# Phase 0 of a two-FFN transformer layer: block 1's mixing ahead of block 2's statistics, the first merged matrices among the r matmuls of the last block

## The reference

```python
x = x + 0.5 * ffn(layernorm(x))          # phases 0 and 3: the same W_r, W_k, W_v, mu_r, mu_k
x = x + attn_layer(layernorm(x))         # phases 1 and 2
x = x + 0.5 * ffn(layernorm(x))

def ffn(z):                              # z_prev: z shifted by one token
    xr = mu_r * z + (1 - mu_r) * z_prev
    xk = mu_k * z + (1 - mu_k) * z_prev
    r = sigmoid(xr @ W_r.T)
    return r * (square(relu(xk @ W_k.T)) @ W_v.T)

def attn_layer(h):                       # 16 heads of 64, causal, low-rank q, k, v (rank 48)
    y = layernorm(h) * ln1_g + ln1_b
    Q = y @ q_U @ q_V + q_b              # k and v likewise
    a = softmax(mask(Q @ K.T / 8)) @ V
    h = h + a @ out_U @ out_V + out_b
    return h + fc2(gelu(fc1(layernorm(h) * ln2_g + ln2_b)))    # low-rank, 1024 to 4096 to 1024
```

## Time and profile before

| | |
|---|---|
| Time, three runs | 1255.38, 1311.06 (median), 1352.09 us |
| The profiled execution: its time | 1256.28 us |
| its span (slowest core) | 1254.6 us |
| spans of the 8 cores | 1245.1 to 1254.6 us |
| PE busy | 1063.0 us (85%) |
| DVE / ACT / POOL busy | 510.5 / 548.5 / 178.5 us |
| The chain that ended last | PE 70%, DMA 9%, DVE 8%, ACT 6%, issue 3% |

### The profile page before, as it was taken

One profiled execution on the slowest core, in us unless ns is written; L12 is line 12 of the kernel. 1 busy time (PEld: TensorE's weight loads), 2 busy tenths in 40 slices (PEclk: granted clock), 3 DMA queues, 4 the chain that ended last, 5 costly groups with the idle time before them and its releaser, 6 DMA issues.

```text
span 1254.6 us, 15373 instructions; the slowest of 8 cores (1245.1 to 1254.6 us)
## 1 busy us (share of the span) xinstructions
PE 1063.0 (85%) x5436; PEld 446.7 (36%) x5436; DVE 510.5 (41%) x975; ACT 548.5 (44%) x662; POOL 178.5 (14%) x165
## 2 busy tenths in 40 slices
PE   2978997999988956889658557699999999999996
PEld 1423443433333312333213222244444444444442
DVE  6378765544343322443227442303303033455421
ACT  2415523466676745767335133443333335432320
POOL 1021133000000010000200201467000000022022
PEclk9989999899999978999869877799999999999998
DMA  9935447422132282200842744595304001521211
GB/s 182 198 128 135 133 97 119 97 61 26 15 31 24 18 137 28 32 10 15 177 105 75 142 60 66 73 203 102 68 1 68 1 1 34 102 76 61 65 68 68
DMA packets 103049, 97.17 MB, mean 77 GB/s; under 512 B 76288, under 2 KB 84608, under 8 KB 101440
## 3 DMA queue, kind: packets, MB, share of 16 engines
q0 software_dynamic: 16656, 44.35, 21.1%
q1 hardware_dynamic: 86320, 51.84, 17.8%
HBM read 96.27 MB, written 16.97 MB: 90 GB/s over the span
## 4 chain that ended last, share of the span: by engine, by line
PE 70%; DMA 9%; DVE 8%; ACT 6%; issue 3%; SPq 1%; POOL 1%; POOLq 0%; ACTq 0%; DVEq 0%
PE ub L836 9%; PE db L1309 9%; PE db L1275 8%; PE db L352 8%; PE db L378 7%; PE db L366 7%; PE sd L939 5%; PE ct L974 5%; PE ub L844 4%; DMA lg<-l_d 3%; ACT AT L949 3%; PE db L1262 3%; DMA r_d<-rg 3%; PE db L1288 2%; PE db L1248 2%
## 5 line engine op out<-in xcount | busy, mean ns | idle before, releaser
L949 ACT ACTIVATE AT<-sd 128x1024 bf16<-128x1024 f32 (+1 forms) x320 | 265.2, 897 | 176.5 <-PE sd L939 176.5
L1352 ACT ACTIVATE HM<-db,csts 128x512 bf16<-128x512 f32 x128 | 80.8, 684 | 139.1 <-PE db L1275 139.1
L974 PE MATMUL ct<-AT,VA 128*64 128x512 bf16 (+3 forms) x640 | 91.1, 363 | 49.3 <-DVE AT L956 49.2
L939 PE MATMUL sd<-Qr,Kr 64*128 64x512 bf16 (+3 forms) x640 | 96.0, 353 | 31.9 <-ACT AT L949 31.4
L1309 PE MATMUL db<-HM,f2U 128*128 128x512 bf16 x512 | 120.3, 379 | 1.7 <-ACT HM L1352 1.7
L1275 PE MATMUL db<-P,f1V 128*128 128x512 bf16 x512 | 120.3, 379 | 0.0
L1248 PE MATMUL db<-Wo,CN 128*128 128x512 bf16 x256 | 62.4, 408 | 19.8 <-DVE S L1394 10.4
L1309 PEld LDWEIGHTS db<-HM,f2U 128*128 128x128 bf16 x512 | 49.9, 98 | 62.6 <-issue 3.3
L1275 PEld LDWEIGHTS db<-P,f1V 128*128 128x128 bf16 x512 | 50.1, 98 | 60.4
L352 PE MATMUL db<-XKa,wk 128*128 128x512 bf16 x256 | 59.0, 393 | 10.7 <-DVE XKa L465 10.6
L836 PE MATMUL ub<-x1T,Wq 128*128 128x512 bf16 x256 | 63.8, 394 | 0.1
(11 more groups left out here) (144 smaller groups left out, 1265.1 us busy)
## 6 DMA issues: line engine op xcount, KB each, us to landing
xs<-X SPq DMA_DIRECT2D x4, 2048.0 KB, 9.6
S<-xs SPq DMA_DIRECT2D x16, 512.0 KB, 12.5
S<-xs POOLq DMA_DIRECT2D x16, 512.0 KB, 32.3
x_out<-S SPq DMA_DIRECT2D x16, 512.0 KB, 2.6
wr<-wrT POOLq DMA_DIRECT2D x4, 1024.0 KB, 17.7
X<-x_in SPq DMA_DIRECT2D x2, 2048.0 KB, 12.2
rb<-r_d SPq DMA_DIRECT2D x64, 64.0 KB, 4.4
f1V<-fc1V POOLq DMA_DIRECT2D x16, 256.0 KB, 16.6
```

The lines of the kernel that those rows point to most:

```text
L939: m = pe.matmul(SD[q % 2][:, TB * s + off:TB * (s + 1)], Kr[p % 2][64 * s:64 * s + 64, 128 * i:128 * (i + 1)], Qr[p % 2][64 * s:64 * s + 6 ...
L949: act.activation(c3(AT[q % 4])[:, :, off:TB], c3(SD[q % 2])[:, :, off:TB], AF.Exp, scale=0.125)._wait_ge(a_qk, q + 1).then_inc(a_exp, 1)
L974: m = pe.matmul(CT[k % 2][64 * s:64 * s + 64, off:TB], VA[p // 4][:, 512 * i + 64 * h:512 * i + 64 * (h + 1)], AT[q % 4][:, TB * s + off:T ...
L1352: m = act.activation(HM[i % 4][:, TB * e:TB * (e + 1)], DB[job_db[("H", b, i)]][:, TB * e:TB * (e + 1)], AF.Gelu_apprx_tanh, bias=scol("fc ...
```

## The change

Three things.

1. DVE, end of block 0: product 1 of block 0 moves into `dve_mix_k` of block 1, behind the difference, and the four statistics A of block 2, which stood two and two around the mixing, move behind products 2 and 3 and `dve_mix_r` of block 1.
2. The units G, qb and Wq of pair 0 are taken out of `prelude` into a list `early`, which PE does between the r tiles of block 3 and DVE evicts ahead of the products of block 3. v tile 1 of block 3, in whose bank UB lies, waits for their evictions. What is left of `prelude` is Q and K of block 0 first, then the four V.
3. DVE's `dve_aff1(NB - 2)`, of block 2, moves from behind the products of block 3 to ahead of them.

Nothing is computed that was not computed before, and no DMA is moved in SP's or POOL's list.

```diff
-    def dve_mix_k(dve, F, f, b):
+    def dve_mix_k(dve, F, f, b, kv=None):
...
         dve.tensor_copy(h1, Z[:, :, TB - 1:TB]).then_inc(F.mx, 1)
+        if kv:
+            dve_kv(dve, F, f, b - 1, kv)
...
             for t in range(4):
                 pe_r(pe, F0, f0, b, t)
+                if b == NB - 1:
+
+                    for u in early[2 * t:2 * t + 2]:
+                        pe_unit(pe, u)
...
             for t in range(4):
+                if b == NB - 1 and t == 1:
+                    pe.wait_ge(u_ev, len(early))
                 pe_v(pe, F0, f0, b, t)
...
                 dve_aff1(dve, b - 2)
-            for t in range(4):
+            if b == NB - 1:
+                for u in early:
+                    dve_unit(dve, u)
+                dve_aff1(dve, NB - 2)
+            if b == 0:
+
+                dve_kv(dve, F0, f0, 0, 0)
+                for k in range(4):
+                    dve.wait_ge(d_tr[k], 16 * (group("A", 1) + 1))
+                dve_mix_k(dve, F0, f0, 1, 1)
+            for t in range(2 if b == 0 else 0, 4):
                 dve_kv(dve, F0, f0, b, t)
-                if b == 0 and t == 1:
-                    dve_mix(dve, 1, dve_mix_k)
-                if b + 2 < NB and t < 2:
+                if b == 1 and t < 2:
...
             if b == 0:
                 dve_mix(dve, 1, dve_mix_r)
-        dve_aff1(dve, NB - 2)
-        for u in prelude[:3]:
+                for k in range(4):
+                    dve_stats_a(dve, 2, k)
+        for u in prelude[:2]:
             dve_unit(dve, u)
         dve_stats_b(dve, NB - 1, 3)
-        for u in prelude[3:5]:
+        for u in prelude[2:4]:
             dve_unit(dve, u)
         dve_rs_b(dve, NB - 1)
-        for u in prelude[5:]:
+        for u in prelude[4:]:
             dve_unit(dve, u)
...
-    prelude = [("G", 0), ("G", 1), ("V", 0, 0), ("qb",), ("Wq", 0, 0), ("Wq", 0, 1), ("V", 0, 1),
-               ("Q", 0, 0), ("K", 0, 0), ("V", 0, 2), ("V", 0, 3)]
+
+    early = [("G", 0), ("G", 1), ("qb",), ("Wq", 0, 0), ("Wq", 0, 1)]
+    prelude = [("Q", 0, 0), ("K", 0, 0)] + [("V", 0, t) for t in range(4)]
...
         elif g == 0:
+            pe.wait_ge(F0.relu, 16)
+        if g == len(early):
             pe.wait_ge(F0.kv, 16)
```

More of the change, by code:

```diff
@@ L778, in build_program @@
     order, unit_no = [], {}
-    for u in prelude + [u for s in slots for u in s]:
+    for u in early + prelude + [u for s in slots for u in s]:
         unit_no[u] = len(order)
```

## The result

The changed kernel is slower by less than a per cent. It stands to the kernel before as 1.0066 (95% interval 1.0034 to 1.0099), with a median of 1262.55 us (1260.70 to 1264.93); timed a second time, beside other kernels, it stood at 1.0025 (1.0003 to 1.0047). The kernel before ran beside it at 1253.33 and 1255.38 us; its executions of 1311.06 and 1352.09 us were in a slower state that comes and goes with either kernel, and every ratio here leaves such executions out. The forecast was 1256 us in 1247 to 1265, a change of −0.4 us (−4.6 + 4.2). The range held the time and the change is far under 2%, as forecast, but the sign was wrong: both intervals lie above 1, so the loss is real, 3.1 us by the second timing and 8.3 by the first.

A forecast was written before the change was run, and what follows sets the result against it. PE was taken as the bound, busy 85% of the span, so a change pays only where PE idles or runs at its lower clock. 1256.3 − 4.6 + 4.2 gave 1256 us, range 1247 to 1265.

The forecast's parts named there:

- Place one: Block 0 to block 1: DVE's new order brings the third r tile from 108.70 to 104.1, a gain of 4.6 us.
- The early units: G, q bias and Wq among block 3's r tiles: together at most 1.6 us of PE, swallowed by its later wait.
- The hold of block 2's transposes: Before block 3's products: with vU's load in flight, the last transpose lands at 207.8 in the old clock; DVE's scale and shift waits.
- the first rival: Block 2's transposes are not held: no PE wait in block 3's v, marker 2.2 us earlier, 1249.5 us; chance 0.17.
- v tile 2 and the clock: Block 3: PE waits 5.0 us before v tile 2, low clock costs 1.4, last product comes 8.0 us later.
- my two bounds: Clock cost after PE's wait before v tile 2 of block 3: between 0 and 1.4 us, with 1.4 taken.
- the sum: Whole kernel: 1256.3 us profiled, minus 4.6 gained at place one, plus 4.2 lost at place two, gives 1256 us.
- the second rival: Clock stays low: v tiles 2 and 3 of block 3 take 6.9 us each, 1263.5 us in all; chance 0.15.
- The marker: Fifth V unit after block 3, held by DVE's scale and shift of block 3: 242.1 in the old clock, 2.8 us later.
- the third rival: Block 3's last transposes fall on its spill: marker moves by some 2.5 us, 1258.5 us in all; chance 0.13.
- Behind the marker: From the fifth V unit on: after PE's 6.7 us wait, the low clock costs 1.4 us more.
- place two: End of block 3, from its r tiles to the fifth V unit: early units and moved scale and shift, loss 4.2 us.

The follow-up runs named there:

- e8: Changed kernel with the moves of e4 and e6, two block 2 statistics in the POOL wait, block 3's last statistics and ACT's second V filling reordered; 1247.81 us, ratio 0.9862.
- e4: Changed kernel, but POOL issues the load of vU only after the transposes of block 2 have landed; ratio 0.9967 to the kernel before.
- e10: Changed kernel, but PE computes v tile 1 of block 3 twice, in the time in which it waits; ratio 1.0022 to the kernel before.
- e5: Changed kernel, but SP issues the spill of block 3 behind the transposes of block 3 instead of ahead; ratio 1.0034 to the kernel before.
- e6: Changed kernel, but DVE's scale and shift of block 3 moves to the fourth step of the attention phase; ratio 0.997 to the kernel before.
- e11: Kernel before with the block 0 part of the change alone, plus block 3's scale and shift in the fourth attention step; ratio 0.9956.

## Why the prediction was right or wrong

- **Place one.** Right in mechanism, 0.8 us small. Forecast 4.6 us, measured 5.4 at the reciprocal on the mean of the cores and 5.36 at the third r tile (108.70 to 103.34). The 19.8 us from XK to the reciprocal came out as forecast (70.04 to 89.87); most of the 0.8 lies in what had been allowed on top. The transposes did not hold DVE at all (the difference follows the first product at 61.82), and XK was ready at 70.04 and not at 70.6. That PE's k moves by 10.5 and only half of it lasts was right, with the statistics as the reason: e8 puts two of them back into the wait for POOL and gets 2.8 us more. The clock's price on the second r tile (5.43 us) was hidden, as forecast.
- **The early units.** Right: 0.61, 0.34, 0.38 and 0.39 us of PE, no wait for their loads. r of block 3 took 14.9 us with them (179.31 to 194.22) and 13.8 without, and that 1.1 us went into the wait.
- **The hold of block 2's transposes.** Right in cause and size: last issue 200.7, DVE on at 203.55, against 207.8 − 4.6 = 203.2. e4 shows the load of vU to be the cause. The rule of the Trainium skill ("DMA: Bandwidth & Descriptors", section "Queues, rings and completion order") that a DMA engine takes turns between its queues would by my reading have let them through. Here the slowest landed 14.8 us after its issue with the load ahead, and 2.8 us after it in e4 without, so in this case the measurement decides against the first rival, which I gave 0.17.
- **v tile 2 and the clock.** The first step that failed, a term too small. I took 1.4 us for the low clock, the upper of my two bounds, from a tile of 4.95 us in the earlier trace rows whose clock was back within it. After a wait of 6.22 us this one took 6.4, at 0.50 until 213: 2.9 us, outside both bounds, and 2.2 on the mean of the cores. The wait was longer too, 6.22 us (5.8 on the mean) and not 5.0: v had come forward by more than forecast, while DVE went on about when forecast (203.55, put down 203.2). So block 3's loss up to the last product was 9.5 us (−5.4 to +4.1) where the sum had 8.0. Of the second rival one tile came, not two: 1.5 us more than forecast on this core, where it had 5.5. e10 shows the price by taking it away.
- **The marker.** The second step that failed, and the larger: an overlap put at nothing. The sum had 8.6 us from the start of the last normalization to scale and shift of block 3; it is 10.7, since the spill, 8 us later in the old clock, is now in flight when these transposes go out. (The 8.6 also takes 3.3 us as the longest landing in the earlier trace rows; that is the median, the longest is 3.8. e5 measures 8.2 with no spill in the way.) I had named the collision as the third rival, with 2.5 us and a chance of 0.13; e5 measures 2.5, and the sign that I gave for it, an issue over 2 us, came with 3371 ns. Its two times were in my own sum, both moved, and I left the collision out of it. By the sum the marker stood at 237.5 (242.1 − 4.6); it came at 240.66.
- **Behind the marker** I put 1.4 us for the clock. The fifth V unit took 2.72 us where it had taken 1.46; between the eviction of the second Q and the first context copy 2.0 were lost.
- **The sum.** Forecast −4.6 + 2.8 + 1.4 = −0.4, measured +3.2 at the first context copy, on the mean of the cores: 3.6 us apart. Place one gave 0.8 more than forecast, v of block 3 cost 1.5 more, the way from the last product to the last normalization 0.4 less, from there to the eviction of the second Q 2.7 more (2.1 of it the collision; for the other 0.6, the one core that I had read stood that much above the mean there before, 10.3 against 9.7 us), and behind it 0.6 more. Every wait stood where it was forecast; what failed is the size of the clock's price and the collision that was left out. That the time fell into the range is no merit of the sum: the range reached from the first rival to the second, and the extra gain of place one hid part of the loss.

What I did not ask: why PE's marker should depend on scale and shift of block 3 at all. It is an instruction in DVE's list that nobody needs before the seventh step, ahead of one that PE needs at once. e6 shows that moving it is worth 6.2 us in the changed kernel, more than place one gained and nearly what place two lost; e11 shows that it is worth nothing where DVE does not wait there.

## What to carry to other kernels

An instruction that waits for a transfer holds all that stands behind it in its engine's list: before moving it forward, read when that transfer lands, not when its source is ready, and put it just ahead of its first reader. When a change shifts two transfers by different amounts, work out whether they now overlap, and put that into the sum, not among the rivals. And where gains and losses of 4 us cancel to "no change", a term that is 2 us off decides the sign: then the sign is not known.

## What the runs showed of the hardware

- Transposes issued by SP were held by a load that POOL had issued before them: an issue of 11.0 to 11.8 us and landings up to 14.8 us with 1536 KB in flight, 1.2 and 2.8 us without it (e4). The load landed at 199.4 in the changed kernel (issued at 180.01, 19.4 us), the last transpose was issued at 200.7. A 2048 KB copy on SP's own queue, issued 6.6 us before, cost them 2.5 us (e5). By what means a transfer in flight holds an issue, no run here shows.
- The granted clock after a wait came back at different times: within a tile of 4.95 us after 6.55 us of waiting, within one of 5.43 us after 8.65 us, only after 6 us (207 to 213) following 6.22 us. For the wait before v tile 2, 5.2 to 6.8 us long, the eight cores of the changed kernel lost 1.5 to 2.9 us. After waits of 1.6 to 2.9 us (e10) it stayed at 1.00 on six cores and fell on two, whose waits, 2.00 and 2.67 us, were not the longest. Repeating 16 matmuls in the wait was cheaper than leaving PE idle.
